# One change to a transformer block kernel: the router reads x minus its mean, and the deviation joins at the logits

## What is computed

```python
mod = (silu(c) @ wmod)                       # six rows: sa, ca, ga, sb, cb, gb
h = layernorm(x) * (1 + ca) + sa
x = x + ga * attention(h, w_qkv, w_out)      # 16 heads of 64, causal over the 2048 tokens
h = layernorm(x) * (1 + cb) + sb
logits = h @ Wr.T + br                       # 8 experts
expert_idx = argmax(logits)
y = relu(h @ W1[e].T + b1[e]) @ W2[e].T + b2[e]
x = x + gb * y                               # y of the chosen expert
```

## Time and profile before

| | |
|---|---|
| three timed runs, us | 986.17, 985.71, 983.54; median 985.71 |
| profiled execution, its own time | 979.31 us |
| its span in the profile | 977.5 us |
| PE busy in the span | 949.9 us (97%) |
| DVE, ACT, POOL busy | 710.1, 675.8, 110.3 us |

### The profile page before, as it was taken

One profiled execution on the slowest core, in us unless ns is written; L12 is line 12 of the kernel. 1 busy time (PEld: TensorE's weight loads), 2 busy tenths in 40 slices (PEclk: granted clock), 3 DMA queues, 4 the chain that ended last, 5 costly groups with the idle time before them and its releaser, 6 DMA issues.

```text
span 977.5 us, 19704 instructions
## 1 busy us (share of the span) xinstructions
PE 949.9 (97%) x6851; PEld 746.1 (76%) x6851; DVE 710.1 (73%) x2363; ACT 675.8 (69%) x1245; POOL 110.3 (11%) x125
## 2 busy tenths in 40 slices
PE   4999999999999999999999999999999999999797
PEld 3678777777777777777777777777777777878697
DVE  6987658784887758784887668874887578986564
ACT  3877658675877768666875768666766677764485
POOL 0200011000100010000100010000100010202244
PEclk9999999999999999999999999999999999999899
DMA  3011100110011100110011000110010000005220
GB/s 82 16 32 26 31 16 20 50 26 20 15 31 26 31 18 18 50 27 20 15 32 50 15 15 13 49 26 20 15 31 18 12 8 11 27 14 175 67 64 27
DMA packets 56003, 30.79 MB, mean 31 GB/s; under 512 B 12455, under 2 KB 53203, under 8 KB 55906
## 3 DMA queue, kind: packets, MB, share of 16 engines
q1 hardware_dynamic: 54658, 27.41, 10.5%
q0 software_dynamic: 1248, 2.13, 0.7%
HBM read 18.21 MB, written 11.77 MB: 31 GB/s over the span
## 4 chain that ended last, share of the span: by engine, by line
PE 96%; DVE 2%; DMA 1%; SPq 0%; ACT 0%; issue 0%; POOLq 0%; POOL 0%; DVEq 0%; ACTq 0%
PE ps L812 27%; PE ps L843 25%; PE ps L825 25%; PE ps L791 5%; PE ps L795 3%; PE ps L856 3%; PE ps L967 2%; PE ps L978 2%; DMA x_sb<-in_L_attn_x_dram 0%; PE ps L942 0%; PE ps L896 0%; PE ps L939 0%; PE ps L958 0%; PE ps L765 0%; DVE k_both L1168 0%; DVE q_both L1164 0%
## 5 line engine op out<-in xcount | busy, mean ns | idle before, releaser
L1032 ACT ACTIVATE probs<-probs,neg_max 128x128 f32<-128x128 f32 (+15 forms) x256 | 309.0, 1210 | 98.0 <-DVE neg_max L1192 96.3
L812 PE MATMUL ps<-k_both,q_both 128*128 128x512 f32 (+2 forms) x1280 | 360.9, 398 | 2.1 <-DVE q_both L1164 1.1
L825 PE MATMUL ps<-ident,probs 128*128 128x128 f32 x2176 | 297.4, 273 | 0.2
L1040 ACT COPY pT<-ps 128x512 f32<-128x512 f32 (+1 forms) x428 | 227.6, 565 | 87.4 <-PE ps L825 81.2
L825 PEld LDWEIGHTS ps<-ident,probs 128*128 128x128 f32 x2176 | 254.7, 140 | 42.4 <-issue 9.9
L1185 DVE TENSOR_SCALAR_CACHE_REDUCE probs<-ps 128x512 f32<-128x512 f32 (+1 forms) x384 | 247.2, 665 | 10.3 <-PE ps L812 8.7
L843 PE MATMUL ps<-pT,v_sb 128*64 128x256 f32 (+1 forms) x2304 | 250.0, 370 | 0.0
L812 PEld LDWEIGHTS ps<-k_both,q_both 128*128 128x128 f32 x1280 | 208.5, 190 | 50.3 <-issue 27.6
L843 PEld LDWEIGHTS ps<-pT,v_sb 128*64 128x64 f32 x2304 | 157.4, 137 | 80.6 <-issue 9.2
L708 POOL CAST k_both<-k_both 64x1024 fp32r<-64x1024 f32 x64 | 66.5, 1038 | 746.3 <-DVE k_both L1168 744.2
L1188 DVE CUSTOM_DVE_ANT_0 probs<-ps,causal 128x256 f32<-128x256 f32 (+3 forms) x256 | 130.6, 510 | 2.1 <-PE ps L812 1.2
(11 more groups left out here) (143 smaller groups left out, 569.2 us busy)
## 6 DMA issues: line engine op xcount, KB each, us to landing
x_sorted<-blank SPq DMA_DIRECT2D x19, 458.5 KB, 5.1
rinv_b<-spread_rows SPq DMA_DIRECT2D x128, 64.0 KB, 2.6
spread_rows<-rinv_rows SPq DMA_DIRECT2D x256, 0.5 KB
probs<-in_L_ffn_W_dram SPq DMA_DIRECT2D x1, 2048.0 KB, 11.9
w_pair<-in_L_attn_w_qkv_dram SPq DMA_DIRECT2D x24, 64.0 KB, 2.2
hT<-x_sorted SPq DMA_DIRECT2D x23, 65.5 KB, 1.8
x_sb<-in_L_attn_x_dram SPq DMA_DIRECT2D x4, 256.0 KB, 4.3
wo_pair<-in_L_attn_w_out_dram SPq DMA_DIRECT2D x8, 64.0 KB, 1.9
```

What stands on the lines that cost most here:

```text
L812: m = pe.matmul(ps_ring[:, s.bank, 0:w], q_split[r % 2][:, q0:q0 + P], k_split[r % 2][:, part, k0:k0 + w], start=(part == 0), stop=(part = ...
L825: m = pe.transpose(ps_turn[:, n % TURN_BANKS, P * r:P * r + P], probs[:, g % 2, r, j * P:j * P + P], ident[:])
L1032: act.activation(row, row, ACT.Exp, bias=neg_max[:, g, r:r + 1], accum_out=row_sum[:, g, r:r + 1]).then_inc(exp_done, 1)
L1040: act.copy(pT[:, n % PT_SLOTS, lo:BANK], ps_turn[:, n % TURN_BANKS, lo:BANK]).then_inc(turn_taken[n % TURN_BANKS], 1)
```

## The change

The router no longer gets the normalised rows. *fresh* only subtracts the mean; a new DVE step *rstds* makes 1/deviation, the same thirteen small instructions, behind it. *mod2* becomes a plain copy. *route* loses the bias matmul and multiplies by `wr_scaled` = Wr times (1 + cb). *pick* first makes `scores_of` = logits times 1/deviation plus `logit_0`, one instruction for each tile, and then goes on as before. `logit_0` = br + sb times Wr is made once, early in the attention, by a new PE step *const* (two matmuls in a ring bank) and a new DVE step *consts*. SP reads two row numbers ahead of the scatters' wait instead of four. The table of the planner gets the new kinds and durations.

```diff
-    EARLY_STARTS = 4
+    EARLY_STARTS = 2
...
+        if kind == "pick":
+            return max(at("route", p, g), at("rstds", p, g))
...
-                "mod2": 240.0 + 530.0 * n, "pick": 800.0 + 1000.0 * n, "slots": 1200.0, "ends": 3300.0,
+                "mod2": 240.0 + 530.0 * n, "pick": 800.0 + 1700.0 * n, "slots": 1200.0, "ends": 3300.0,
...
+                elif s.kind == "const":
+                    pe.wait_ge(sort_made, 3)
+                    pe.wait_ge(br_in, 16)
+                    b_bank, b_use = plan.bank_of("small", 0, 0)
+                    pe.wait_ge(bank_free[b_bank], b_use + 1)
+                    pe.wait_ge(bank_free[s.bank], s.use)
+                    pe.matmul(ps_ring[:, s.bank, 0:NE], ones[:], br_row[:], start=True, stop=False, skip_group_check=True)
+                    pe.matmul(ps_ring[:, s.bank, 0:NE], ones[:], wr_shift[:], start=False, stop=True,
+                              skip_group_check=True).then_inc(bank_full[s.bank], 1)
...
-                    pe.matmul(ps_ring[:, s.bank, 0:n * NE], ones[:], br_row[:].unsqueeze(1).broadcast_to([P, n, NE]),
-                              start=True, stop=False, skip_group_check=True)
...
-                                      wrT[:], start=False, stop=True, skip_group_check=True)
+                                      wr_scaled[:], start=True, stop=True, skip_group_check=True)
...
-                    act.activation(hT[:, first * P:(first + n) * P], ps_ring[:, bank, 0:n * P], ACT.Identity,
-                                   bias=mod[:, 3:4], scale=mod[:, 7:8]).then_inc(bank_free[bank], 1)
+                    act.copy(hT[:, first * P:(first + n) * P], ps_ring[:, bank, 0:n * P]).then_inc(bank_free[bank], 1)
...
                 elif s.kind == "fresh":
+                    first, n = parts_of(p)[s.key[1]]
+                    for t in range(first, first + n):
+                        m = dve.tensor_scalar(x_normed[:, t, :], x_sb[:, t, 0:E], mean_var[:, t, 0:1], None, ALU.subtract)
+                    m.then_inc(norm_ready, 1)
+                elif s.kind == "rstds":
...
-                    for t in range(first, first + n):
-                        m = dve.tensor_scalar(x_normed[:, t, :], x_sb[:, t, 0:E], x_sb[:, t, MEAN:MEAN + 1],
-                                              x_sb[:, t, RSTD:RSTD + 1], ALU.subtract, ALU.mult)
-                    m.then_inc(norm_ready, 1)
...
-                    link(dve.tensor_reduce(top[:, 0:n], logits, AX.X, ALU.max))
                     for t in range(n):
-                        m = dve.scalar_tensor_tensor(out=is_top[:, t, :], in0=logits[:, t, :], scalar=top[:, t:t + 1],
-                                                     in1=expert_no[:], op0=ALU.is_equal, op1=ALU.mult)
+                        m = dve.scalar_tensor_tensor(out=scores_of[:, t, :], in0=logits[:, t, :],
+                                                     scalar=x_sb[:, first + t, RSTD:RSTD + 1], in1=logit_0[:],
+                                                     op0=ALU.mult, op1=ALU.add)
                     m.then_inc(bank_free[bank], 1)
                     dve.wait_ge(bank_free[bank], use + 1)
+                    link(dve.tensor_reduce(top[:, 0:n], scores_of[:, 0:n, :], AX.X, ALU.max))
+                    for t in range(n):
+                        m = dve.scalar_tensor_tensor(out=is_top[:, t, :], in0=scores_of[:, t, :], scalar=top[:, t:t + 1],
+                                                     in1=expert_no[:], op0=ALU.is_equal, op1=ALU.mult)
+                    link(m)
```

More of the change, by code:

```diff
@@ L86 @@
 class Plan:
-    IN_RING = ("score", "out", "proj", "back", "small", "turn2", "route", "rank", "total", "wturn")
-    EMPTIES = {"top": "score", "lo": "proj", "value": "proj", "add": "out", "resid": "back", "smalls": "small",
+    IN_RING = ("score", "out", "proj", "back", "small", "const", "turn2", "route", "rank", "total", "wturn")
+    EMPTIES = {"top": "score", "lo": "proj", "value": "proj", "add": "out", "resid": "back", "smalls": "small", "consts": "const",
                "mod2": "turn2", "pick": "route", "slots": "rank", "ends": "total", "wtake": "wturn"}
@@ L108, in __init__ @@
                     add=norms, resid=ends,
-                    small=[(0, 0)], smalls=[(0, 0)], fresh=ends, turn2=ends, mod2=ends, route=ends, pick=ends,
+                    small=[(0, 0)], smalls=[(0, 0)], const=[(0, 0)], consts=[(0, 0)], fresh=ends, rstds=ends, turn2=ends, mod2=ends, route=ends, pick=ends,
                     rank=ends, slots=ends, total=[(PAIRS - 1, 0)], ends=[(PAIRS - 1, 0)],
@@ L142 @@
     CLOSING = ("out", "back", "turn2", "route", "rank", "total")
-    KINDS = dict(pe=("score", "turn", "pv", "out", "proj", "back", "small", "turn2", "route", "rank", "total", "wturn"),
+    KINDS = dict(pe=("score", "turn", "pv", "out", "proj", "back", "small", "const", "turn2", "route", "rank", "total", "wturn"),
                  act=("hi", "value", "take", "exp", "mod2", "wtake"),
-                 dve=("norm", "sum", "lo", "add", "resid", "top", "take", "smalls", "fresh", "pick", "slots", "ends"))
+                 dve=("norm", "sum", "lo", "add", "resid", "top", "take", "smalls", "consts", "fresh", "rstds", "pick", "slots", "ends"))
     FIRST = dict(act=("hi", "value"), dve=("sum", "norm", "lo"))
@@ L211, in ready @@
         if kind in self.IN_RING:
-            return max(at({"turn2": "fresh", "route": "mod2", "rank": "pick"}[kind], *key), self.ring_free())
+            return max(at({"const": "smalls", "turn2": "fresh", "route": "mod2", "rank": "pick"}[kind], *key), self.ring_free())
         return at({"hi": "proj", "lo": "hi", "add": "out", "resid": "back", "smalls": "small", "mod2": "turn2",
-                   "pick": "route", "slots": "rank", "ends": "total", "wtake": "wturn"}[kind], *key)
+                   "consts": "const", "rstds": "fresh", "slots": "rank", "ends": "total", "wtake": "wturn"}[kind], *key)
     def get_from(self, p, g):
@@ L273, in took @@
                 return 866.0 + switch
-            n = 1.0 if kind in ("small", "total") else parts_of(key[0])[key[1]][1] / 4.0
-            return n * {"out": 862.0, "back": 436.0, "small": 200.0, "turn2": 436.0, "route": 440.0,
+            n = 1.0 if kind in ("small", "const", "total") else parts_of(key[0])[key[1]][1] / 4.0
+            return n * {"out": 862.0, "back": 436.0, "small": 200.0, "const": 500.0, "turn2": 436.0, "route": 440.0,
                         "rank": 700.0, "total": 400.0}[kind] + switch
@@ L284, in took @@
         return {"hi": 1190.0, "lo": 1384.0, "value": 580.0, "sum": 360.0, "norm": 160.0 + 530.0 * n,
-                "add": 160.0 + 590.0 * n, "resid": 500.0 + 1700.0 * n, "smalls": 200.0, "fresh": 2400.0 + 1030.0 * n,
-                "mod2": 240.0 + 530.0 * n, "pick": 800.0 + 1000.0 * n, "slots": 1200.0, "ends": 3300.0,
+                "add": 160.0 + 590.0 * n, "resid": 500.0 + 1700.0 * n, "smalls": 200.0, "consts": 300.0, "fresh": 200.0 + 1030.0 * n, "rstds": 2400.0,
+                "mod2": 240.0 + 530.0 * n, "pick": 800.0 + 1700.0 * n, "slots": 1200.0, "ends": 3300.0,
                 "wtake": 590.0}[kind]
@@ L344, in choose_pe @@
                  ("out", True), ("back", True), ("rank", True), ("turn2", True), ("route", True), ("total", True),
-                 ("small", True), ("score", early), ("turn", True), ("score", True), ("pv", True),
+                 ("small", True), ("const", True), ("score", early), ("turn", True), ("score", True), ("pv", True),
                  ("proj", due <= PROJ_LEAD + 2), ("wturn", True)]
@@ L416, in adaln_block @@
         wrT = sb("wrT", [P, NE])
+        wr_scaled = sb("wr_scaled", [P, NE])
+        wr_shift = sb("wr_shift", [P, NE])
+        logit_0 = sb("logit_0", [P, NE])
+        scores_of = sb("scores_of", [P, TPC, NE])
         b1_cols = sb("b1_cols", [P, NE * FT])
@@ L1252, in _ @@
                     dve.tensor_copy(b1_cols[:], ps_ring[:, bank, 0:NE * FT])
-                    dve.tensor_copy(wrT[:], ps_ring[:, bank, NE * FT:NE * FT + NE]).then_inc(bank_free[bank], 1)
-                elif s.kind == "fresh":
+                    link(dve.tensor_copy(wrT[:], ps_ring[:, bank, NE * FT:NE * FT + NE]))
+                    dve.tensor_scalar(wr_scaled[:], wrT[:], mod[:, 7:8], None, ALU.mult)
+                    dve.tensor_scalar(wr_shift[:], wrT[:], mod[:, 3:4], None, ALU.mult).then_inc(bank_free[bank], 1)
+                elif s.kind == "consts":
+                    bank, use = plan.bank_of("const", *s.key)
+                    dve.wait_ge(bank_full[bank], use + 1)
+                    dve.tensor_copy(logit_0[:], ps_ring[:, bank, 0:NE]).then_inc(bank_free[bank], 1)
+                    dve.wait_ge(bank_free[bank], use + 1)
+                elif s.kind == "fresh":
+                    first, n = parts_of(p)[s.key[1]]
[3 more added lines that the diff above has]
+                elif s.kind == "rstds":
                     first, n = parts_of(p)[s.key[1]]
```

2 lines of the change are left out of this document (removed).

## The result

The changed kernel takes 989.01 us (median of 18 timed runs, 985.88 to 994.81), the kernel before 985.62 (18 runs, 983.28 to 987.22). The ratio is 1.0035, with a 95% interval of 1.0026 to 1.0045: 3.4 us slower. 987.5 was forecast, in a range of 984.0 to 990.9. The time lies in the range, but just past the 0.3% that I called no change, where the likeliest case had stood. The upper end of that range had been drawn for DVE as the bound in pair 7, which did not happen. So part of the hit is luck.

A forecast was written before the change was run, and what follows sets the result against it. PE was taken to bound the attention, with a PE-DVE chain at the close. Terms +2.0 + 0.3 - 0.6 + 0.7 - 0.65 = +1.75 us on the timed median 985.71 gave 987.5 us, range 984.0 to 990.9.

The forecast's parts named there:

- the likeliest case: Whole kernel: measured time within about 0.3% (3 us) of no change, chance 0.66.
- DVE as the bound in pair 7: Rival, close of parts 0 to 2: later picks also on the path, score runs at upper bound; +4.2, 989.9 us, chance 0.22.
- The score runs and const: Pairs 1 and 2: PE waits for DVE in longer runs of ring steps, +2.0; const and consts themselves +0.3.
- the eleventh step: Last ring step between pv and pair 1's first turn: DVE needs 4.9 us, PE 3.8, so PE waits 1.1.
- The bias matmul: Its removal from four routes in the attention saves 0.14 us each on PE: -0.6.
- The pick of part 0: Pair 7: the new pick instruction for each tile goes straight onto PE's path, +0.7.
- the picks of parts 1 and 2: Pair 7: the rank behind the pick shows no wait, so 0 each, bound +0.7 each.
- The close: Last part, up to the first normalised tile: shorter chain and two fewer row numbers, mostly taken back; -0.65, bounds -0.3 and -1.3.
- the last weight copy: Before the loop: ACT's copy, ending at 919.24, holds DVE's first expert copy; only 0.1 us earlier after the change.
- The clock in the loop: Loop start: low clock left as is; rival either way, 986.6 or 988.4 us, chance 0.10.
- Free score runs: Rival, pairs 1 and 2: DVE enters the eleven steps well ahead, no cost; -0.25, 985.5 us, chance 0.16.

The follow-up runs named there:

- the const step alone: Kernel before with only the const and consts steps added, their result unused: 987.5 us against 985.19, ratio 1.0022.
- late-scatter version: All POOL scatters of x moved behind the last pv: changed kernel 997.52 us against 986.15, kernel before 992.28 against 983.98.
- early copies: Changed kernel with DVE's four expert copies waiting only for the copies of W1, not every ring bank: 987.81 us against the changed kernel's 989.19.
- no const step: Changed kernel without const and consts in the plan, logit_0 made in the first route's bank: 985.62 us against 985.19 of the kernel before, ratio 1.0008.
- the second profile of before: Kernel before, unchanged, profiled once more: 986.03 us, span 984.2.

## Why the prediction was right or wrong, point by point

**The score runs and const: right, +2.3 predicted, +2.5 in the profile (a to b, 302.75 against 300.2), 2.2 in the times of the const step alone.** By the arithmetic the eleventh step can't start before 4.9 us. In the rows the first starts at 150.90, and the eleventh 0.58 us ahead of the turn, at 155.87: 4.97 us later, where PE's own work is 3.8 by the prediction's rates. The second run is longer than was said, thirteen ring steps in a row. The first starts at 259.17 and the last at 265.15, 5.98 us later, where the same rates give 4.4. That makes 1.2 and 1.6 us, of which 2.5 are left at b; 1.1 each had been forecast. const's two matmuls stand 0.1 us apart.

**The bias matmul: mis-sized, -0.6 predicted, -0.2 found (b to c).** Only part 0's shows. The others lie in d to e, where waits of over a microsecond hide a difference of 0.14.

**The pick of part 0: right in size, +0.7 predicted, +0.6 to 0.7 found, with a side effect that I missed.** The wait in front of out came out as said, 0.56 us (c to d, 2.24 against 1.68). PE has little to do around that rank, and it idles half a microsecond longer than before (0.19, 0.40 and 0.35 us in the second profile, where 0.35 stood). In six of eight profiles of kernels with the new pick the granted clock then falls to its lower level, 1.2 GHz, for some 3 us, in none of the six with the old one. The late-scatter version of the changed kernel, and that of the kernel before:

```profile
830.00:832.00 2.00, 1.25 (x10) 1.13 (x10) 1.97 (x8) 0.00 (x0) 0.00 (x0) 1.00 0.00 0
832.00:834.00 2.00, 2.00 (x4) 0.86 (x5) 1.71 (x11) 1.46 (x2) 0.00 (x0) 0.52 0.01 4
834.00:836.00 2.00, 2.00 (x10) 1.76 (x9) 1.97 (x7) 0.12 (x1) 0.00 (x0) 0.62 0.01 1
```
```profile
830.00:832.00 2.00, 1.97 (x8) 1.09 (x9) 1.72 (x10) 1.46 (x2) 0.00 (x0) 1.00 0.00 0
832.00:834.00 2.00, 2.00 (x18) 1.86 (x18) 1.96 (x7) 1.17 (x3) 0.00 (x0) 1.00 0.02 5
834.00:836.00 2.00, 2.00 (x15) 1.73 (x14) 1.97 (x8) 2.00 (x5) 0.00 (x0) 1.00 0.00 0
```

Without scatters d to e is 75.20 against 73.87, and from d to turn2 of part 1 it is 15.96 against 14.56: the clock costs 1.4 us there. With scatters that is not added. Where the clock falls, the wait of 1.5 us for part 0's scatters near 839 doesn't come, and the stretch takes 16.1 us on the mean in six profiles of the new order, 16.0 in four of the old. The Trainium skill, "TensorE: Matmul & The Clock Gate", Part 1, says that the clock follows PE's recent activity; I had weighed that for the loop alone, and the trace agrees with it here.

**The rest of pair 7: a term that the sum lacked.** d to e is 78.7 us on the mean in four profiles of the old order with scatters, 80.6 in six of the new. Of these 1.9 us 0.1 stand before turn2 of part 1 and 1.8 behind it. The order by itself costs nothing there: without scatters that rest takes 59.2 us in the new order and 59.3 in the old, so the picks of parts 1 and 2 are as free as forecast. With scatters it takes 62.7 on the mean in the old. In the new it takes 63.0 to 63.8 in three profiles and 65.4 to 66.0 in the three others, and the three others are those in which the clock fell a second time, at 863.1, 902.1 or 898.9. The same 36 pv matmuls, in the first profile of the changed kernel, just behind that fall, and in the second, at full clock:

```profile
901.90 5.79 PE L849 MATMUL ps<-pT,v_sb 128*64 128x256 f32 x36
```
```profile
902.99 4.11 PE L849 MATMUL ps<-pT,v_sb 128*64 128x256 f32 x36
```

So the falls go with 2.3 us where they come, in half of the profiles, and 0.6 us are left without them. No profile of the old order has one before the loop. The timed runs agree: the mean granted clock is 0.990 over the 18 of the changed kernel and 0.992 to 0.993 over the 72 of the kernel before that stood beside the experiments. The prediction weighed the clock for the loop alone. What lets it fall in one execution and not in the next, after waits as long (2.08 and 0.79 us with early copies, 2.04 and 0.76 in the first profile of the changed kernel), stays open, and no run held the clock up to price it by itself.

**The close: right, -0.65 predicted, -0.7 to -1.1 found, within its bounds of -0.3 to -1.3.** From e to the end it is 73.1 us on the mean of three profiles with the new close (the changed kernel twice, no const step) and 74.2 on that of three with the old (the kernel before twice, const step alone). One of the old three, the second profile of before, had the long low clock in the loop; the other two have 73.8. The chain gains 2.1 us up to total (9.37 us behind the last pv, 11.5 in the second profile of before) where the prediction had 1.7 to 1.8 at ends. Nearly all of it is lost to the last weight copy, as predicted and as the early copies show. The last weight step comes 0.1 us earlier than in the first profile of before, as forecast, and 0.35 earlier than in the others.

**The clock in the loop.** The first eight matmuls still take 2.08 us, even when PE waits only 3.06. The third tile's took 1.16 us in the earlier trace rows, 1.78 in the second profile of the kernel before and 1.18 and 1.08 in those of the changed one: the moment at which the clock rises does move.

**The rivals.** DVE as the bound in pair 7, at 989.9, gave the nearest time, but by a mechanism that did not happen: the picks of parts 1 and 2 show no such wait. Free score runs are refuted by the const step alone. The terms add up to 2.5 - 0.2 + 0.6 + 1.9 - 1.1 = 3.7 us, against 3.4 measured and 1.75 forecast. Nearly all that the sum missed is the 1.9, and the step that missed it was the base. I noted that the profiled execution was 6.4 us below the median and left it at that. 5.4 of these were waits in the very stretch that the change reorders, so that no row showed how thin PE already was there.

## What to carry to other kernels

When the profiled execution is much shorter than the median of the timed runs, the missing time lies somewhere: find it in a second profile before costing an edit there. Look at the granted clock in every stretch, not only where the kernel ends: waits of half a microsecond to two in a dense stretch went with a fall of the clock in most profiles here, and it cost 1.4 us or more each time that nothing else covered it. A step for work off the path can cost more than the work, if the planner then puts score steps in a row that another engine has to empty; making the constant inside an existing step saved 2.7 us.

## What the runs showed of the hardware

While scatters issued by POOL were in flight, ACT and DVE started copies up to 3 us after PE's work for them was done: d to e was 4 to 7 us longer with twelve scatters there (part of it by the clock), and in one profile not at all. The granted clock fell to 0.5 within two us of a short idle time of PE in the middle of the attention, and was back at 1.00 some 3 us later; in two of the eight profiles with that idle time it did not fall.
